# Multiplying a table of ones on TensorE behind the last attention scores of a one-core macaron block

## The reference, cut to what matters

```python
def _L0_ffn_ref(input, ...):          # 8 experts, 1024 hidden, capacity 512 tokens each
    logits = x @ w_switch + b_switch
    probs = jax.nn.softmax(logits, axis=-1)
    routes = probs.argmax(axis=-1)
    ...
    h = jax.nn.relu(jnp.einsum('ecd,edh->ech', buf_e, w1) + b1[:, None, :])
    y = jnp.einsum('ech,ehd->ecd', h, w2) + b2[:, None, :]
...
x = x + 0.5 * _L0_ffn_ref(_layernorm(x, axis=-1), ...)
x = x + _L0_attn_ref(_layernorm(x, axis=-1), ...)      # 16 heads of 16, softmax over 1024 keys
x = x + 0.5 * _L0_ffn_ref(_layernorm(x, axis=-1), ...)
```

## Time and profile before

| | us |
|---|---|
| median of 3 runs | 2451.97 |
| the three runs | 2451.97, 2429.93, 2452.05 |
| the profiled execution | 2452.92 |
| its span | 2451.1 |
| TensorE busy in the span | 2177.5 (89%) |
| VectorE busy | 1740.6 (71%) |
| ScalarE busy | 1730.3 (71%) |

### The profile page before, as it was taken

The page is one execution under the profiler, slowest core; times in us unless marked ns, Lnnn a source line. Parts: engine busy times, 40 slices in busy tenths (PEclk is TensorE's granted clock), DMA queues, the critical chain, the costliest instruction groups (busy, mean ns, idle before and its releaser), DMA issues.

```text
span 2451.1 us, 36414 instructions
## 1 busy us (share of the span) xinstructions
PE 2177.5 (89%) x12974; PEld 1153.8 (47%) x12974; DVE 1740.6 (71%) x2555; ACT 1730.3 (71%) x3390; POOL 976.2 (40%) x1157
## 2 busy tenths in 40 slices
PE   5749964579999999999999999999999999964997
PEld 5748853344344434434443443444444334224896
DVE  5636754368888888798888778878888988203774
ACT  5846654128888788788878878877887877634663
POOL 3754512271264256239227514832741111112442
PEclk8569986569999999999999999999999999666998
DMA  5725420514235334344333444432362340103431
GB/s 201 264 88 181 152 73 35 103 35 96 54 64 120 58 76 105 71 58 105 97 57 85 101 76 73 90 94 37 84 122 41 78 62 16 51 9 130 139 121 61
DMA packets 144901, 218.29 MB, mean 89 GB/s; under 512 B 32224, under 2 KB 100954, under 8 KB 144464
## 3 DMA queue, kind: packets, MB, share of 16 engines
q1 hardware_dynamic: 135504, 199.01, 34.6%
q0 software_dynamic: 9216, 16.95, 2.0%
HBM read 129.59 MB, written 84.80 MB: 87 GB/s over the span
## 4 chain that ended last, share of the span: by engine, by line
PE 73%; DVE 10%; POOL 5%; ACT 5%; issue 4%; DMA 2%; SPq 0%; POOLq 0%; DVEq 0%; ACTq 0%
PE PS L780 18%; PE PS L764 17%; PE PS L747 11%; PE PS L692 6%; DVE NMX L1302 5%; PE PS L568 4%; PE PS L724 3%; POOL buf L1425 2%; PE PS L661 2%; PE PS L662 2%; PE PS L663 2%; PE PS L645 2%; PE PS L647 2%; PE PS L600 2%; PE PS L646 2%
## 5 line engine op out<-in xcount | busy, mean ns | idle before, releaser
L1302 DVE TENSOR_REDUCE NMX<-PS 128x1 f32<-128x1024 f32 x1024 | 1224.5, 1219 | 300.7 <-PE PS L747 294.9
L998 ACT ACTIVATE PB<-PS 128x512 f32<-128x512 f32 x2048 | 1103.4, 605 | 250.9 <-PE PS L764 243.4
L764 PE MATMUL PS<-QF,KF 51*128 51x512 f32 x2048 | 814.6, 473 | 12.1 <-ACT PB L998 7.4
L747 PE MATMUL PS<-KF,QF 49*128 49x512 f32 x2048 | 725.1, 451 | 47.8 <-DVE NMX L1302 35.6
L764 PEld LDWEIGHTS PS<-QF,KF 51*128 51x128 f32 x2048 | 334.8, 189 | 573.6 <-ACT PB L998 292.8
L780 PE MATMUL PS<-PB,V 128*17 128x512 f32 x4096 | 559.4, 619 | 0.2
L747 PEld LDWEIGHTS PS<-KF,QF 49*128 49x128 f32 x2048 | 315.7, 190 | 181.9 <-DVE NMX L1302 116.1
L1406 POOL TENSOR_TENSOR RS<-VE,NEGH 128x8 f32<-128x8 f32 x24 | 40.2, 1676 | 404.8 <-DVE VE L1096 404.8
L1229 DVE TENSOR_TENSOR HLR<-HL,HHR 128x512 fp32r<-128x512 f32 x128 | 88.7, 693 | 91.8 <-ACT HHR L928 91.8
L661 PE MATMUL PS<-W2H,HLR 128*128 128x256 f32 x512 | 142.8, 279 | 0.0
L663 PE MATMUL PS<-W2H,HHR 128*128 128x256 f32 x512 | 141.5, 276 | 0.0
(11 more groups left out here) (171 smaller groups left out, 3303.5 us busy)
## 6 DMA issues: line engine op xcount, KB each, us to landing
W<-in_w SPq DMA_DIRECT2D x32, 1024.0 KB, 8.1
QF<-qs SPq DMA_DIRECT2D x192, 128.0 KB, 4.7
KF<-qs SPq DMA_DIRECT2D x192, 128.0 KB, 7.5
qs<-HI SPq DMA_DIRECT2D x64, 256.0 KB, 2.1
qs<-R1R SPq DMA_DIRECT2D x64, 256.0 KB, 2.4
buf<-ZT SPq DMA_DIRECT2D x16, 520.0 KB, 9.9
BUF<-buf SPq DMA_DIRECT2D x16, 520.0 KB, 8.4
PX<-x2d SPq DMA_DIRECT2D x8, 1024.0 KB, 5.5
```

The costliest lines, as they stand in the source:

```text
L747: m = e.matmul(PS[:, 2 * i + half, :], QF[k][at:at + ROWS_S, p * SEQ + ti * 128:p * SEQ + ti * 128 + 128], KF[k][at:at + ROWS_S, p * SEQ + ...
L764: e.matmul(PS[:, bank, :], KF[k][at:at + ROWS_ST, p * SEQ + sbk * 128:p * SEQ + sbk * 128 + 128], QF[k][at:at + ROWS_ST, p * SEQ + th * 51 ...
L998: e.activation(PB[j % 3][:, h * 512:(h + 1) * 512], PS[:, place["e", tile], :], ACT.Exp).then_inc(e_out, 1)
L1302: e.tensor_reduce(NMX[:, u % 2, at:at + 1], PS[:, 2 * i:2 * i + 2, :], AX.XY, ALU.max, negate=True).then_inc(s_max, 1)
```

## The change

`again(times)` issues so many matmuls with the table of ones (128 by 128, bf16) as weights and the same table, repeated four times, as 512 moving columns. They write bank 0, which nobody reads after the last maximum. It is called with 3 in each of the steps 512 to 533, behind the step's own matmuls and ahead of `side.run`; with 48 at step 534, behind a wait for `pv_out` (the last copy of bank 7); with 16 at step 552, behind the projections; with 16 at step 573, behind the count; and with 16 more behind a wait for all eight `scat` semaphores. These are 66 + 48 + 16 + 16 + 16 = 162 matmuls. The wait for `s_max` at step 512 is for the last maximum of banks 0 to 3. No other engine's program is changed. Line numbers behind the constants grow by 5, from `between` on by more.

```diff
+AGAIN = (3, 48, 16, 16, 16)
+AGAIN_Y = LAG + LATE
...
+            def again(times):
+                for i in range(times):
+                    e.matmul(PS[:, 0, :], ONES[:, :], ONES[:, :].unsqueeze(1).to_broadcast([128, 4, 128]),
+                             start=True, stop=True)
+
+            def between(c):
+                yield AGAIN_Y
+                e.wait_ge(pv_out, 2 * NU)
+                again(AGAIN[1])
+                yield PROJ_AT[7] + 1
+                again(AGAIN[2])
+                yield LEAVE + 18
+                again(AGAIN[3])
+                for i in range(8):
+                    e.wait_ge(scat[i], 32 * NB)
+                again(AGAIN[4])
...
+                if n == NS:
+                    side.begin(n, between(2 * NB - 1))
...
+                if n == NS:
+                    e.wait_ge(s_max, 32 * NU)
+                if n >= NS and j - LATE < NS:
+                    again(AGAIN[0])
                 side.run(n)
```

## The result

The changed kernel takes 2431.42 us in the median of 20 runs (2427.09 to 2436.59), against 2449.49 of 20 runs of the kernel before (2429.93 to 2452.36). The ratio is 0.9938, with a 95% interval from 0.9921 to 0.9955: between 11 and 19 us less, within 1%. The profiled execution took 2430.24, its span is 2428.4; before it was 2452.92 and 2451.1, so 22.7 us are to be found in the two traces.

What follows compares the result with a forecast made beforehand. The prediction took TensorE at its lower clock to pace the late weighing steps. Gains of 21.2 + 1.3 + 0.5 + 0.3 = 23.3 us off 2452.92 gave 2429.6, less 0.95 for the median: 2428.7 us, range 2418 to 2441.

Steps and rivals of the forecast that it cites:

- the sum: All forecast gains added, from the weighing steps to the experts' start: 21.2 + 1.3 + 0.5 + 0.3 = 23.3 us.
- The step: Weighing step with three ones after the last scores: 2.74 us at 2.4 GHz instead of 4.04 us.
- the three steps of 3.17: First three steps after the weighing at 2103.91, paced by ACT's additional activations: 3.17 us each.
- the tail: From the weighing at 2168.55 to the copy of bank 7: 4.98 us instead of 6.67, gain 1.7.
- The 48: Ones between the copy of bank 7 and the projections: no cost at 2.4 GHz, projections gain 1.3 us (0 to 1.7).
- The 16 behind the projections: Ones in the idle time before the transposes and logits: gain 0.5 us, ends 0 and 3.4.
- The 16 behind the count: Ones after the count, with TensorE's next work 24 us later: cost 0, gain 0.
- The last 16: Ones after the scatters, before the experts' first transposes: gain 0.3 us, from -0.5 to 2.
- Clock up throughout: Rival: clock also stays up through the transposes and into the first expert, 2423.8 us; chance 0.16.
- Held in part: Rival: ones hold the clock only part of the time, five weighing steps taking 5.07 us, total 2440; chance 0.12.
- Loads exposed at 0.19 each: Rival: each matmul of ones shows its weight load, 0.19 us; step 3.31, total 2444; chance 0.04.
- Slower than before: Rival: ones don't count, clock stays down, 16 weighing steps grow from 4.04 to 5.07 us, total 2476; chance 0.06.

Runs made afterwards that it cites:

- the execution of 2420.32: Profiled run of the changed kernel without the ones in the steps, those in the gaps kept; that kernel's median is 2451.24 us, ratio 1.0007.
- Both with 58: Two kernels with 58 matmuls instead of 48 before the projections, one with one full-array matmul a step, one with four 64-row ones: 2427.41 and 2422.01 us.
- filled gaps: Changed kernel with one matmul of ones a step and 58, 30, 16, 16 and 11 in the gaps: 2427.41 us, ratio 0.9882; also combined with four 64-row ones: 2422.01.
- the kernel with ones in the wait: Changed kernel with its three ones a step moved between a step's first weight and the second, which waits for an exponential: 2440.87 us, ratio 0.9927.
- the fp32r table: Changed kernel multiplying the q, k and v weight matrix in fp32r instead of the bf16 ones, in steps and gaps: 2486.53 us, ratio 1.0118.

## Why the prediction was right, and where its sizes were off

**The mechanism held.** In the trace the steps are at 1.00 without a wait, and the rest came as forecast: the copy of YU at 2155.68 instead of 2175.22 (forecast about 2154), the projections 13.65 behind it and 7.17 long (13.7 and 7.1), ones 0.22 apart (0.22 to 0.23), transposes and logits at 0.50. Removing the ones of the steps while keeping those of the gaps removes the gain (1.0007); removing those of the gaps keeps it (0.9946). That the gain is the clock and nothing else of the ones is borne out by the execution of 2420.32, which had the clock without ones in the steps.

**The time came nearer than the sum.** The medians differ by 18.1 us, where the sum has 23.3. The forecast is only 2.7 off since it started from a median of three runs, 2451.97, and that of twenty is 2.5 lower. In the profiled executions (2430.24 against the 2429.6 of the sum) 4.6 us too few up to the copy of YU are made up mostly by 2.9 ahead of the change, which have nothing to do with it, and 1.1 more than forecast behind the count.

**The step was mis-sized**: 3.05 for 2.74, which the prediction itself had named as a sign against it ("if the step isn't near 2.74"). The sum had 0.33 + 0.23 for the two weights behind a weighing and 0.23 + 0.32 for the two ahead; each pair takes 0.66, 0.2 us more for the two. I had read the three weights in 0.73 as spaced by 0.33 and 0.23, and the place of the ones among them as indifferent. It isn't: in a run of three, two start together and the third 0.33 later, and by the code the ones went to the border at which two overlap. The rest is 0.07 for the first of the ones and 0.05 that I had shaved from the sum of 2.79. From the weighing that was at 2103.91 to the one at 2168.55, after takes 48.85 us (16 steps of 3.05) where the forecast had 45.1: 3.8 us. In these, the three steps of 3.17 that ScalarE was to pace were 3.05 like the others. The first two steps behind the last scores, which cost nothing in the sum, lose 0.5, and the tail 0.3.

**The 48**: 1.7 against 1.3; the idle of 2.47 did not cost the clock in this execution. That is luck: of the nine profiled executions with 48 matmuls of ones (bf16 or fp32r) or bf16 data there, four have projections of 7.17 (behind 1.75 to 2.47 of idle) and five of 8.61 to 10.22 (behind 2.34 to 3.36). Both with 58 have 7.17.

**The 16 behind the projections**: 0 against 0.5. The clock fell at 2182.5, 1.2 us ahead of the transposes, as the working said it might. The filled gaps show what there was to gain: 1.0 and 0.3 in two executions, not the upper end of 3.4. Both traces agree with "TensorE: Matmul & The Clock Gate", Part 4, of the Trainium skill, by which transposes don't engage the full clock: in the changed kernel their stage stayed at 0.50, and with the filled gaps, with 1.99 of 2.00 busy, the clock fell to 0.50 in their midst. Logits of 8 columns lie between them, so the rows don't say which of the two it is.

**The 16 behind the count**: 0 against 0. **The last 16**: 0.65 + 0.76 against 0.3. They raise the clock at 2220.0, 3 us into them, so the transposes behind take 1.10 instead of 1.94, which I hadn't counted; they do so in all traces with these ones. The experts then start at 0.50 all the same and rise 2.9 us in instead of 4.4. In this I had doubted too much: in six of nine such executions they start at 1.00, and the full 2.0 of the working is about what it brings (199.6 to 200.5 to the end, where the two traces without ones in the gaps have 201.8 and 202.7).

**The rivals.** Clock up throughout: no, it fell in two gaps. Held in part: not in the steps of the changed kernel, nor with one a step; the kernel with ones in the wait has a dip of 3.4 us. Loads exposed at 0.19 each: no; 0.22 per further one, 0.32 for the first. Slower than before: not with ones, but the fp32r table is that case, dearer than forecast (5.71 a step for 5.07, ratio 1.0118).

**What the forecast overlooked** is that the kernel before sometimes keeps its clock. A part of its runs needs no ones and loses 0.46 a step by them. That fits the changed kernel's fastest run (2427.09), which is no better than the fastest of the 33 of before (2425.71).

## What to carry to other kernels

Where a stretch runs with a busy TensorE at its lower clock, try the filler in the smallest amount that holds it, and sweep one, two and three: here one was enough, and each more cost 0.22 us a step. Look for a place where the filler costs least: in the half of the array that the neighbouring matmul leaves free four matmuls of ones cost nothing; three over the whole array cost 0.24 us a step in the wait and 0.46 between the steps. An idle stretch filled only in part left the clock to chance (four of nine executions kept it); filled up to the next work it was kept in both that were profiled, which is too few to be sure. And look at the spread of the runs before: a clock lost in most runs and kept in some shows as two groups.

## What the runs showed that I had not expected

- The same instructions seem to keep the clock in some executions and lose it in most: 6 of 33 runs of the kernel before and 3 of 12 with ones in the gaps alone lie 11 to 31 us below the median; of these, one was profiled, and it had the clock.
- A TensorE whose records show 10.00 of 10.00 us busy stayed at 1.2 GHz for 92 us, with full-array fp32r matmuls in every step; in the steps without attention weights it rose.
- A 64-row matmul of ones and a 51-row weight in the other half of the array start in the same 0.01 us, and four such per step lengthen it by nothing.
- Full-array matmuls of ones with 512 columns start 0.22 us apart in bf16 and 0.23 in fp32r when many stand in a row; three between the attention weights cost 0.76 and 0.90.
